# Row-tiled scatter of two images, a streamed router, and a top-2 mixture shared by VectorE, ScalarE and GpSimd

## The chip, the core and the metric

The kernel runs on one core of one Trainium2 chip as one program. The metric is the device time of the whole execution in microseconds (us). Before the change it is 9376.89 us, the median of three runs (9366.43 to 9382.52). Names of the engines as the profile has them: PE is TensorE's matmul side and PEld its weight loads, DVE is VectorE, ACT is ScalarE, POOL is GpSimd, and SP is the engine that issues most of the DMAs.

## The reference

Four layers of a network run over 4 images of 48 x 48 positions with 128 channels, 9216 tokens in all. Each layer adds a mixer of positions and then a per-token part to the running `x`. The change touches two kinds of per-token part.

Layers 1 and 2 end in an expert-choice layer: 64 experts each take a weighted sum over an image's tokens (`topv` is zero but for 8 tokens of each expert), run it through a small network, and give their outputs back to the tokens with the same weights. This giving back is the scatter:

```python
weighted = jnp.einsum('beo,bke->bkeo', out, topv).reshape(Bn, K * E, O)
outputs = outputs.at[jnp.arange(Bn)[:, None], flat_idx].add(weighted)
```

Layer 3 ends in a mixture of 8 experts, of which every token uses the two with the highest router probability:

```python
router_probs = jax.nn.softmax(x @ router_w + router_b, axis=-1)
top_p, top_i = jax.lax.top_k(router_probs, K)
top_p = top_p / jnp.sum(top_p, axis=-1, keepdims=True)
expert_out = jnp.einsum('bnd,edc->bnec', x, expert_w) + expert_b
gathered = jnp.take_along_axis(expert_out, top_i[..., None], axis=2)
return jnp.einsum('bnk,bnkc->bnc', top_p, gathered)
```

The input of both is the layer-normed `x`, and all arithmetic is float32.

## The kernel before, in words

`metaformer` runs the stages one after another. A stage is one or more blocks; at the end of a block all engines meet and the block's semaphores are cleared, so nothing of one block runs beside the next. `X`, the running `x` of layers 1 to 3, stays on chip as 72 tiles of 128 tokens by 128 channels (36 groups of two tiles).

**The scatter** (`scatter_tokens`, called by `expert_choice` in layers 1 and 2). `weights` holds, for two images at a time, 64 rows (experts) of one image in partitions 0 to 63 and 64 rows of the other in 64 to 127. SP moves the experts' outputs into `rows` in the same layout, 16 DMAs (L2287). DVE adds the second bias to the rows of two images (L2307) and lets PE begin. PE then works image by image, in 5 steps per image: a step fills one PSUM bank with 4 tiles (2 in the last) by matmuls with only 64 rows of contraction (L2299). DVE adds each bank to `X` (L2313), 20 additions. PE may run 8 banks ahead.

**The mixture** (`top2_experts`) has these blocks:

- `load_all` fetches the identity, the router and the expert weights, and `bias_rows` fetches the router's and the experts' biases in a load block of its own, then a second block makes from them a row in high and low parts and a matrix of ones, so that a bias can be added by a matmul.
- `norm_and_turn` norms the tokens and leaves them transposed in `XT` (channels by tokens).
- Router block `mr`, 18 turns with 4 tiles each: ACT copies 512 columns of `XT` to `stage` (L3035), PE makes for each tile a matmul with the 128 x 128 token tile as stationary operand and the router's 8 columns as moving one (L3045), and one for the bias (L3046), and DVE copies 32 columns to `gates` (L3055).
- `route` turns `gates` into the normed probabilities of each token's two best experts; all others become 0.
- Mixture block `me`, 36 turns with 2 tiles each: ACT rounds the tokens to `high` (L3079), POOL makes `low` as the rest (L3071), PE makes for each tile and each half of the 8 experts (4 experts by 128 channels, one bank) three matmuls, high by high, high by low and low by high (L3094), and one for the bias (L3095). DVE then takes 8 times, once for each expert, `x = ps * gate + x` per tile (L3112), 16 instructions a turn. Two sets of 4 banks alternate, and so do two buffers each of `high` and `low`.

The order inside a block is the order of the code on each engine. Loops with `Fori` are loops on the chip and others are written out.

## Time and profile before

| | us |
|---|---|
| median of the runs | 9376.89 |
| profiled execution, its own time | 9381.17 |
| its span, first to last instruction | 9378.6 |
| first scatter, PE's first to DVE's last instruction | 6648.6 to 6678.0 |
| second scatter | 8624.0 to 8653.5 |
| load and making of the bias rows | 9083.0 to 9092.7 |
| norm and transposes for the mixture | 9092.7 to 9126.5 |
| router block | 9128.1 to 9175.0 |
| route | 9175.8 to 9193.6 |
| mixture block, ACT's first to DVE's last instruction | 9194.5 to 9361.4 |
| store of the result | 9362.4 to 9378.6 |

The profile is of one execution. Its times are microseconds from the start of the span. Busy time of an engine doesn't say that the engine bounds a stage; for that one reads who waited for whom there. The mean of an instruction (in ns) holds its own start-up, part of which lies beside the instruction before it, so instructions that follow each other closely start at a smaller distance than their duration.

### The profile page before, as it was taken

Reading aid. Unit: us, or ns where it says so; the run is one execution under the profiler, and the core shown is the slowest. Engines: PE = TensorE matmul, PEld = TensorE weight load, DVE = VectorE, ACT = ScalarE, POOL = GpSimd, SP = SyncE. Lnnn points to the kernel's source line nnn. Section 1 sums busy time; section 2 is a strip of 40 time slices with the busy share of each in tenths; the row PEclk is TensorE's granted clock in tenths of the full one; section 3 lists DMA queues with packets and bytes.
Section 4 is the critical chain, followed back from the end, with each engine's and each line's share of the span. In section 5 each row is a group of like instructions: output and inputs, shape, how many; then the busy total and the mean of one; then the engine's idle time right before and its main releaser. Section 6 shows DMA issues by size and latency. Waiting matters only on the chain. (4 is left out here: it accounts for less than half of the span.)

```text
span 9378.6 us, 167204 instructions
## 1 busy us (share of the span) xinstructions
PE 7377.9 (79%) x63268; PEld 4812.3 (51%) x63268; DVE 6500.1 (69%) x8252; ACT 4637.2 (49%) x8709; POOL 4163.0 (44%) x2920
## 2 busy tenths in 40 slices
PE   5877778777778777875799999388499989995667
PEld 3444444444444344444788888166355555553455
DVE  7999899998999799993166555232376656633447
ACT  4666566665666466652156555124224444452431
POOL 4999599995999499983300000000100000010001
PEclk8999999999999999995699999699679999997778
DMA  4555355553555355544332333621300010003000
GB/s 145 165 165 165 92 177 164 163 151 119 165 165 165 91 175 165 165 128 151 134 74 60 89 86 86 160 71 45 143 21 16 21 36 16 16 1 148 21 23 20
DMA packets 470862, 976.30 MB, mean 104 GB/s; under 512 B 127918, under 2 KB 226549, under 8 KB 452983
## 3 DMA queue, kind: packets, MB, share of 16 engines
q1 hardware_dynamic: 469098, 938.10, 33.6%
q10 hardware_dynamic: 960, 27.53, 1.1%
q8 instruction: 501, 8.21, 0.4%
q14 instruction: 303, 2.47, 0.1%
HBM read 822.05 MB, written 114.81 MB: 100 GB/s over the span
## 5 line engine op out<-in xcount | busy, mean ns | idle before, releaser
L892 POOL TENSOR_TENSOR ss_work<-ss_dtu,ss_ringb 128x768 f32<-128x768 f32 x1536 | 2759.6, 1822 | 260.0 <-POOLq L59 256.6
L754 PE MATMUL ss_ps<-ss_work,ss_ident 128*128 128x512 f32 (+1 forms) x6144 | 2307.9, 521 | 615.5 <-POOL ss_work L902 600.0
L754 PEld LDWEIGHTS ss_ps<-ss_work,ss_ident 128*128 128x128 f32 x6144 | 1201.0, 203 | 1503.5 <-issue 1319.0
L876 DVE TENSOR_TENSOR_SCAN ss_work<-ss_ps,ss_last,ss_work 128x768 f32<-128x768 f32 x1024 | 1808.6, 1800 | 64.2 <-ACT ss_ps L807 53.2
L807 ACT ACTIVATE ss_ps<-ss_dt,ss_a_neg 128x768 f32<-128x768 f32 x1536 | 1374.6, 895 | 288.1 <-DVE ss_work L876 270.9
L861 DVE TENSOR_TENSOR ss_work<-ss_work,ss_ps 128x1152 f32<-128x1152 f32 x768 | 1019.0, 1327 | 1.2 <-ACT ss_ps L815 1.2
L2655 DVE TENSOR_REDUCE at_top<-at_ps 128x1 f32<-128x384 f32 x1512 | 728.1, 546 | 402.5 <-PE at_ps L2573 402.3
L2636 ACT ACTIVATE at_probs<-at_ps 128x768 f32<-128x768 f32 x864 | 653.6, 808 | 660.4 <-PE at_ps L2592 659.4
L876 DVE TENSOR_TENSOR_SCAN ss_work<-ss_ps,ss_work 128x768 f32<-128x768 f32 x512 | 878.1, 1742 | 51.4 <-issue 18.0
L1409 DVE COPY mb_mix<-mb_ps 128x432 f32<-128x432 f32 x1088 | 634.4, 632 | 400.5 <-PE mb_ps L1432 400.4
L1499 ACT ACTIVATE mb_mix<-mb_ps 128x432 f32<-128x432 f32 x1088 | 612.6, 619 | 435.0 <-PE mb_ps L1432 429.0
L902 POOL TENSOR_TENSOR ss_work<-ss_work,ss_ringc 128x384 f32<-128x384 f32 x768 | 772.4, 1006 | 22.1 <-DVE ss_work L876 22.1
L1432 PE MATMUL mb_ps<-mb_taps,mb_mats 105*128 105x216 f32 x4352 | 668.1, 298 | 28.8 <-DMA mb_mats<-fq_mats 24.8
L2602 PE MATMUL at_ps<-at_probs,at_v 128*64 128x384 f32 x3456 | 663.5, 506 | 0.0
L1432 PEld LDWEIGHTS mb_ps<-mb_taps,mb_mats 105*128 105x128 f32 x4352 | 549.0, 196 | 128.3 <-issue 78.1
L2558 POOL COPY at_inv<-at_kept 32x384 f32<-32x384 f32 x80 | 39.9, 499 | 1224.3 <-ACT at_kept L2641 1222.7
L1449 PE MATMUL mb_ps<-mb_mix,mb_bins 128*8 128x64 f32 x29376 | 522.3, 221 | 30.7 <-issue 30.5
L1492 POOL COPY mb_bins<-mb_bins_by 128x432 f32<-128x432 f32 x34 | 20.3, 596 | 1182.6 <-PE mb_ps L1449 1049.6
L2573 PE MATMUL at_ps<-at_packs 96*128 96x384 f32 x1512 | 496.9, 379 | 19.6 <-DMA at_packs<-at_high 19.1
L813 ACT ACTIVATE ss_ps<-ss_ringc 128x512 f32<-128x512 f32 x768 | 462.7, 603 | 83.3 <-DVE ss_work L861 80.1
L2592 PE MATMUL at_ps<-at_packs 128*128 128x384 f32 x1728 | 453.0, 355 | 53.2 <-PEq L59 40.2
L1449 PEld LDWEIGHTS mb_ps<-mb_mix,mb_bins 128*8 128x8 f32 x29376 | 420.2, 90 | 94.8 <-issue 36.1
(554 smaller groups left out, 9917.5 us busy)
## 6 DMA issues: line engine op xcount, KB each, us to landing
ss_ringb<-scan_rows SPq DMA_DIRECT2D x768, 384.0 KB, 3.6
ss_ringc<-scan_rows SPq DMA_DIRECT2D x768, 384.0 KB, 3.9
c_w<-in_l_ffn_w SPq DMA_DIRECT2D x52, 1024.0 KB, 12.3
mb_mats<-fq_mats ACTq DMA_DIRECT2D x8, 3360.0 KB, 17.3
at_packs<-at_high SPq DMA_DIRECT2D x64, 288.0 KB, 5.5
fq_mats<-fq_mats_high SPq DMA_DIRECT2D x8, 2048.0 KB, 9.8
fq_bins<-tb_out SPq DMA_DIRECT2D x68, 216.0 KB, 1.9
mb_bins_by<-fq_bins SPq DMA_DIRECT2D x34, 432.0 KB, 3.9
```

What stands on the lines that cost most here:

```text
L754: return pe.matmul(acc[:, d * WIN + a:d * WIN + e], ident[:, :], weighed[:, t % DEEP, d, a:e], start=n == 0 and e - a == 512, stop=n == NS ...
L807: act.activation(decay[d], dt[:, i % 2, d, :], ACT.Exp, scale=a_neg[:, SECTIONS[i][0], d, n:n + 1]).then_inc(s["decayed"], 1)
L861: dve.tensor_tensor(weighed[:, t % DEEP, :, 0:SPLIT], hid[:, t % DEEP, :, 0:SPLIT], bc(spread_c[:, None, :], [P, D2, SPLIT]), ALU.mult).th ...
L876: dve.tensor_tensor_scan(hid[:, t % DEEP, d, ::step], decay[d][:, ::step], drive[:, t % DEEP, d, ::step], start, ALU.mult, ALU.add).then_i ...
L892: pool.tensor_tensor(drive[:, t % DEEP, d, :], dtu[:, t // NST % 2, d, :], ringb[:, t % RING, :], ALU.mult).then_inc(s["driven"], 1)
L902: pool.tensor_tensor(weighed[:, t % DEEP, :, SPLIT:WIN], hid[:, t % DEEP, :, SPLIT:WIN], bc(ringc[:, t % RING, None, SPLIT:WIN], [P, D2, W ...
L1409: copy(*fill_part(h, n)).then_inc(sem, 1)
L1432: ins = pe.matmul(ps[:, n % 4, e * COLS:(e + 1) * COLS], mats[:, first:first + P], taps[:, c % 2, :], start=True, stop=True, skip_group_ch ...
L1449: ins = pe.matmul(ps[32 * g:32 * g + 8, 4 + y % 2, at:at + HALF_E], bins[:, c % 2, n, 1 - m:3 - m, :].rearrange("p m b -> p (m b)"), mix[: ...
L2602: ins = pe.matmul(acc[64 * h:64 * h + 64, 0:R], v[:, j, 2 * pair + h, :, :].rearrange("p a d -> p (a d)"), probs[:, n % 4, h, :], start=j ...
L2636: act.activation(probs[:, n % 4, :, :], ps[:, 2 * (n % 2):2 * (n % 2) + 2, 0:R], ACT.Exp).then_inc(s["weighed"], 1)
L2655: dve.tensor_reduce(top[:, bass.ds(tile + h * NT_, 1), u], ps_bank(ps, 5 + g % 3)[:, 0:R], AX.X, ALU.max).then_inc(s["reduced"], 1)
```

## The change

**Scatter.** The loop goes over pairs of images. In each step one matmul for the lower image (partitions 0 to 63) and one for the upper (64 to 127) alternate, and they fill two different banks. DVE's additions come in the same order. Their number and sizes stay.

**Bias rows.** `bias_rows` is not called for the mixture. The router's bias is fetched to all partitions by one DMA in the first load, and DVE adds it to the logits. The experts' biases come through the gates: 16 small DMAs put them on the diagonal blocks of `blocks` (16 tiles by 8 experts in the partitions), the gates of 16 tiles are transposed by PE, and one matmul then makes gate times bias for 4 tiles.

**Router.** `logits_of_tokens` turns the operands round: the router's 8 columns are stationary and 512 tokens stream past them. Four such matmuls go to four column positions (PSUM partitions 0, 32, 64, 96) of one bank. ACT copies the bank, PE transposes it in 4 pieces, and DVE picks the 8 useful columns out of each 32 and adds the bias. Before it starts, DVE clears 5 banks and `blocks`. SP sends the 16 DMAs in this block.

**Mixture.** `mix_experts` first transposes the gates, then runs 18 bias matmuls, which DVE adds to `X`. Then come 36 pairs of tiles. The bias matmuls are gone from the loop. DVE takes 4 of the 8 experts as before. ACT multiplies the other 4 with their gates into `scaled`, POOL adds these up in two steps to `sums`, and DVE adds `sums` to `X` one pair later. All is written out, no loop on the chip is left.

The diff, cut to its core; the lines it removes from `top2_experts` stand in the listing above (`spread` gives an access pattern that reads the same row into all 128 partitions; `layout` gives the experts' biases as 8 rows of 128 and no longer as one row):

```diff
-                for j in range(B * 5):
-                    b, n = j // 5, j % 5
-                    half = slice(b % 2 * NE, b % 2 * NE + NE)
+                for i in range(NPAIR * 5):
+                    pair, n = i // 5, i % 5
                     if n == 0:
-                        pe.wait_ge(s["rows_ready"], b // 2 + 1)
-                    if j >= 8:
-                        pe.wait_ge(s["added"], j - 7)
+                        pe.wait_ge(s["rows_ready"], pair + 1)
+                    if i >= 4:
+                        pe.wait_ge(s["added"], 2 * (i - 3))
                     for m in range(4 if n < 4 else 2):
-                        ins = pe.matmul(ps[:, j % 8, m * C:(m + 1) * C], tile_of(weights[half, b // 2, :], 4 * n + m), rows[half, b // 2, :], start=True, stop=True)
+                        for h in range(2):
+                            half = slice(h * NE, h * NE + NE)
+                            ins = pe.matmul(ps[:, (2 * i + h) % 8, m * C:(m + 1) * C], tile_of(weights[half, pair, :], 4 * n + m), rows[half, pair, :], start=True, stop=True)
...
+        router_b, blocks = sb("router_b", [P, NX]), sb("blocks", [P, P // NX, C])
         XT = sb("xt", [P, T])
-        stage = sb("stage", [P, 2, 4, P])
-        load_all(nc, "moe_load", [(ident[:, :], w["ident"]), (router[:, :], w["router"]), (ew[:, :], w["ew"])])
-        ones, (router_b, eb) = bias_rows(nc, ctx, "moe_b", [w["router_b"], w["eb"]])
+        load_all(nc, "moe_load", [(ident[:, :], w["ident"]), (router[:, :], w["router"]), (ew[:, :], w["ew"]), (router_b[:, :], spread(w["router_b"], NX))])
...
+        logits_of_tokens(nc, ps, XT, router, router_b, ident, gates, blocks, w["eb"])
+        route(nc, gates)
+        mix_experts(nc, ctx, ps, X, XT, ident, gates, blocks, ew, ew_high, ew_low)
...
+def logits_of_tokens(nc, ps, XT, router, router_b, ident, gates, blocks, eb):
...
+    with nc.sbuf_tensor("lg_kept", [P, GROUPS_T, CHUNK], F32) as kept:
...
+            @block.tensor
+            def _(pe):
+                pe.wait_ge(s["blank"], 2)
+                for n in range(GROUPS_T):
+                    for c in chunks_in(n):
+                        at = 32 * (c % GROUP)
+                        ins = pe.matmul(ps[at:at + NX, n, :], router[:, :], XT[:, CHUNK * c:CHUNK * (c + 1)], start=True, stop=True, skip_group_check=True)
+                    ins.then_inc(s["made"], 1)
+                for n in range(GROUPS_T):
+                    pe.wait_ge(s["kept"], n + 1)
+                    if n >= 3:
+                        pe.wait_ge(s["gated"], n - 2)
+                    for t in range(GROUP):
+                        ins = pe.transpose(ps[:, GROUPS_T + n % 3, t * P:(t + 1) * P], kept[:, n, t * P:(t + 1) * P], ident[:, :])
+                    ins.then_inc(s["turned"], 1)
             @block.scalar
             def _(act):
+                for n in range(GROUPS_T):
+                    act.wait_ge(s["made"], n + 1)
+                    act.activation(kept[:, n, :], ps[:, n, :], ACT.Copy).then_inc(s["kept"], 1)
             @block.vector
             def _(dve):
+                dve.memset(ps[:, 0:GROUPS_T, :], 0.0).then_inc(s["blank"], 1)
+                dve.memset(blocks[:, :, :], 0.0).then_inc(s["blank"], 1)
+                for n in range(GROUPS_T):
+                    g = len(chunks_in(n))
+                    dve.wait_ge(s["turned"], n + 1)
+                    out = gates[:, 16 * n:16 * n + GROUP * g, :].rearrange("p (g t) e -> p t g e", t=GROUP)
+                    source = ps[:, GROUPS_T + n % 3, :].rearrange("p (t g e) -> p t g e", t=GROUP, g=GROUP)[:, :, 0:g, 0:NX]
+                    dve.tensor_tensor(out, source, bc(router_b[:, None, None, :], [P, GROUP, g, NX]), ALU.add).then_inc(s["gated"], 1)
+            @block.sync
+            def _(sp):
+                sp.wait_ge(s["blank"], 2)
+                for k in range(P // NX):
+                    sp.dma_start(blocks[NX * k:NX * (k + 1), k, :], eb).then_inc(s["diagonal"], 16)
+                sp.wait_ge(s["diagonal"], 16 * (P // NX))
...
+def mix_experts(nc, ctx, ps, X, XT, ident, gates, blocks, ew, ew_high, ew_low):
+    PAIRS_T, QUADS_T = G, G // 2
...
+    def rows_in(n):
+        return NX * min(16, 2 * G - 16 * n)
+    def quad_bank(i):
+        return ps[:, (GROUPS_T + i) % 8, :]
+    def expert_bank(v, t, n):
+        return ps[:, 4 * (v % 2) + 2 * t + n, :]
...
+        @block.tensor
+        def _(pe):
+            for n in range(GROUPS_T):
...
+                ins = pe.transpose(ps[0:rows, n, 0:P], gates[:, 16 * n:16 * n + rows // NX, :].rearrange("p t e -> p (t e)"), ident[:, :])
+                ins.then_inc(s["turned"], 1)
+            pe.wait_ge(s["kept_t"], GROUPS_T)
+            for i in range(QUADS_T):
+                n, rows = i // 4, rows_in(i // 4)
+                if i >= 8:
+                    pe.wait_ge(s["bias_added"], i - 7)
+                pe.matmul(quad_bank(i), gates_t[0:rows, n, :], blocks[0:rows, 4 * (i % 4):4 * (i % 4) + 4, :].rearrange("p t c -> p (t c)"),
+                          start=True, stop=True, skip_group_check=True).then_inc(s["bias_made"], 1)
+            pe.wait_ge(s["weights_ready"], 1)
+            for v in range(PAIRS_T):
+                pe.wait_ge(s["lowered"], v + 1)
+                for t in range(2):
+                    if v >= 2:
+                        pe.wait_ge(s["freed"], 2 * (v - 2) + t + 1)
+                        pe.wait_ge(s["scaled"], 2 * (v - 2) + t + 1)
+                    elif t == 0:
+                        pe.wait_ge(s["bias_added"], QUADS_T)
+                    for n in range(2):
+                        for turn, (x, m) in enumerate(((high, ew_high), (high, ew_low), (low, ew_high))):
+                            ins = pe.matmul(expert_bank(v, t, n), x[:, v % 2, t, :], m[:, n * 512:(n + 1) * 512], start=turn == 0, stop=turn == 2)
+                        ins.then_inc(s["made"], 1)
+        @block.scalar
+        def _(act):
+            def stage(v):
+                at_least(act, s["made"], 4 * (v - 1))
+                act.activation(high[:, v % 2, :, :].rearrange("c t p -> c (t p)"), XT[:, 256 * v:256 * (v + 1)], ACT.Copy).then_inc(s["staged"], 1)
+            def scale(v, t):
+                act.wait_ge(s["made"], 4 * v + 2 * t + 2)
+                at_least(act, s["halved"], 2 * (v - 2) + t + 1)
+                for e in range(SHARE):
+                    gate = gates[:, 2 * v + t, SHARE + e:SHARE + e + 1]
+                    ins = act.activation(scaled[:, v % 2, t, e, :], expert_bank(v, t, 1)[:, e * C:(e + 1) * C], ACT.Copy, scale=gate)
+                ins.then_inc(s["scaled"], 1)
+            for n in range(GROUPS_T):
...
+                act.wait_ge(s["turned"], n + 1)
+                act.activation(gates_t[0:rows, n, :], ps[0:rows, n, 0:P], ACT.Copy).then_inc(s["kept_t"], 1)
+            act.activation(ew_high[:, :], ew[:, :], ACT.Copy).then_inc(s["cut"], 1)
+            stage(0)
+            stage(1)
+            for v in range(PAIRS_T):
+                scale(v, 0)
+                scale(v, 1)
+                if v + 2 < PAIRS_T:
+                    stage(v + 2)
+        @block.gpsimd
+        def _(pool):
+            def lower(v):
+                pool.wait_ge(s["staged"], v + 1)
+                source = XT[:, 256 * v:256 * (v + 1)].rearrange("c (t p) -> c t p", t=2)
+                pool.tensor_tensor(low[:, v % 2, :, :], source, high[:, v % 2, :, :], ALU.subtract).then_inc(s["lowered"], 1)
+            def add_up(v):
+                for t in range(2):
+                    pool.wait_ge(s["scaled"], 2 * v + t + 1)
+                    pool.tensor_tensor(scaled[:, v % 2, t, 0:2, :], scaled[:, v % 2, t, 0:2, :], scaled[:, v % 2, t, 2:4, :], ALU.add).then_inc(s["own"], 1)
+                for t in range(2):
+                    pool.wait_ge(s["own"], 2 * v + t + 1)
+                    at_least(pool, s["added"], 2 * (v - 2) + t + 1)
+                    pool.tensor_tensor(sums[:, v % 2, t, :], scaled[:, v % 2, t, 0, :], scaled[:, v % 2, t, 1, :], ALU.add).then_inc(s["halved"], 1)
+            pool.wait_ge(s["cut"], 1)
+            pool.tensor_tensor(ew_low[:, :], ew[:, :], ew_high[:, :], ALU.subtract).then_inc(s["weights_ready"], 1)
+            lower(0)
+            for v in range(PAIRS_T):
+                if v + 1 < PAIRS_T:
+                    lower(v + 1)
+                add_up(v)
+        @block.vector
+        def _(dve):
+            def weigh(v):
+                for e in range(SHARE):
+                    for t in range(2):
+                        if e == 0:
+                            dve.wait_ge(s["made"], 4 * v + 2 * t + 1)
+                        else:
+                            dve.wait_ge(s["summed"], 2 * (SHARE - 1) * v + 2 * (e - 1) + t + 1)
+                        out = tiles[:, 2 * v + t, :]
+                        ins = dve.scalar_tensor_tensor(out, expert_bank(v, t, 0)[:, e * C:(e + 1) * C], gates[:, 2 * v + t, e:e + 1], out, ALU.mult, ALU.add)
+                        ins.then_inc(s["summed"] if e < SHARE - 1 else s["freed"], 1)
+            def add_rest(v):
+                for t in range(2):
+                    dve.wait_ge(s["freed"], 2 * v + t + 1)
+                    dve.wait_ge(s["halved"], 2 * v + t + 1)
+                    out = tiles[:, 2 * v + t, :]
+                    dve.tensor_tensor(out, out, sums[:, v % 2, t, :], ALU.add).then_inc(s["added"], 1)
+            for i in range(QUADS_T):
+                dve.wait_ge(s["bias_made"], i + 1)
+                out = tiles[:, 4 * i:4 * i + 4, :].rearrange("p t c -> p (t c)")
+                dve.tensor_tensor(out, out, quad_bank(i), ALU.add).then_inc(s["bias_added"], 1)
+            dve.wait_ge(s["bias_added"], QUADS_T)
+            for v in range(PAIRS_T):
+                weigh(v)
+                if v:
+                    add_rest(v - 1)
```

How this stands in the order of instructions. SP around the mixture's loads; the first column is the line, `moe_` are the mixture's tensors and `in_` those in memory:

```order
 L312 DMA moe_router<-in_l_ffn_router 128x8
 L312 DMA moe_ew<-in_l_ffn_ew 128x1024
-L308 UNCONDITIONAL_BRANCH
-L309 UNCONDITIONAL_BRANCH
-L312 DMA moe_b_raw<-in_l_ffn_router_b 1x8 x2
-L312 DMA moe_b_raw<-in_l_ffn_eb 1x1024 x2
+L312 DMA moe_router_b<-in_l_ffn_router_b 128x8
 L308 UNCONDITIONAL_BRANCH
 L166 UNCONDITIONAL_BRANCH
+L3081 UNCONDITIONAL_BRANCH
+L3085 DMA moe_blocks<-in_l_ffn_eb 8x128 x16
+L3047 UNCONDITIONAL_BRANCH
```

One load block of four DMAs is gone, one DMA joins the first load, and 16 DMAs come into the router's block.

PE from the end of the norm on, in the kernel before (router block, then mixture block, both loops):

```order
L257 MATMUL moe_ln_ps<-moe_ident,moe_xn 128x128 x72
L165 UNCONDITIONAL_BRANCH
L3037 UNCONDITIONAL_BRANCH
L3040 UNCONDITIONAL_BRANCH
L3040 ISA
L3045 MATMUL moe_ps<-moe_router,moe_stage 128x8
L3046 MATMUL moe_ps<-moe_b_bias,moe_b_ones 128x8
...
L3094 MATMUL moe_ps<-moe_ew_high,moe_stage_high 128x512
L3094 MATMUL moe_ps<-moe_ew_low,moe_stage_high 128x512
L3094 MATMUL moe_ps<-moe_ew_high,moe_stage_low 128x512
L3095 MATMUL moe_ps<-moe_b_bias,moe_b_ones 128x512
```

And PE at the same place in the changed kernel:

```order
L257 MATMUL moe_ln_ps<-moe_ident,moe_xn 128x128 x72
L165 UNCONDITIONAL_BRANCH
L3048 UNCONDITIONAL_BRANCH
L3054 MATMUL moe_ps<-moe_xt,moe_router 8x512 x18
L3061 MATMUL moe_ps<-moe_ident,lg_kept 128x128 x20
L3047 UNCONDITIONAL_BRANCH
L3114 UNCONDITIONAL_BRANCH
L3118 MATMUL moe_ps<-moe_ident,moe_gates 128x128 x4
L3118 MATMUL moe_ps<-moe_ident,moe_gates 64x128
L3125 MATMUL moe_ps<-moe_blocks,moe_gates_t 128x512 x18
L3138 MATMUL moe_ps<-moe_ew_high,moe_stage_high 128x512
L3138 MATMUL moe_ps<-moe_ew_low,moe_stage_high 128x512
```

The router's 144 matmuls became 18 with 20 transposes behind them, and the bias matmuls moved out of the mixture's loop to a stretch ahead of it.

POOL in the mixture's loop of the changed kernel, two pairs of tiles (before, its loop holds L3071 alone):

```order
L3173 TENSOR_TENSOR moe_stage_low<-moe_xt,moe_stage_high 128x256
L3178 TENSOR_TENSOR moe_scaled<-moe_scaled 128x256 x2
L3182 TENSOR_TENSOR moe_sums<-moe_scaled 128x128 x2
L3173 TENSOR_TENSOR moe_stage_low<-moe_xt,moe_stage_high 128x256
L3178 TENSOR_TENSOR moe_scaled<-moe_scaled 128x256 x2
```

The `low` part of a later pair now stands behind the sums of an earlier one.

## Rows read from the trace of the kernel before

**Rows 1.** Windows: length, busy (count) of PE, PEld, DVE, ACT, POOL; clock, DMA.

```profile
6648.50:6678.00 29.50, 29.02 (x144) 28.73 (x144) 12.66 (x22) 0.00 (x0) 0.00 (x0) 0.50 0.01 3
...
9128.00:9175.00 47.00, 45.87 (x216) 45.78 (x216) 3.45 (x18) 11.23 (x18) 0.00 (x0) 0.51 0.00 0
...
9198.80:9204.20 5.40, 5.36 (x13) 4.21 (x14) 0.00 (x0) 0.00 (x0) 0.58 (x1) 0.50 0.00 0
9205.50:9361.40 155.90, 139.29 (x560) 101.99 (x558) 151.60 (x576) 14.13 (x34) 25.12 (x34) 1.00 0.00 0
```

**Rows 2.** Chain that ended last, its shares by line, 9205.5 to the end.

```profile
by line: DVE x L3112 47.6%; issue 26.4%; DVEq L3111 11.5%; DVEq L3112 2.9%; DVEq L3102 1.0%; DVEq L3104 0.4%
```

**Rows 3.** Timeline of the first scatter; start, length, engine, line, what, [idle before, releaser].

```profile
6641.86 10.06 SPq L2287 DMA_DIRECT2D c1s_rows<-c_outs  x16
...
6653.19 0.29 DVE L2307 TENSOR_TENSOR c1s_rows<-c1s_rows,c1s_b 128x128 f32<-128x128 f32 x1 [4.69 <-DMA c1s_rows<-c_outs]
6653.40 1.87 DVE L2313 TENSOR_TENSOR x<-x,c1s_ps 128x512 f32<-128x512 f32 x3
...
6670.63 0.42 DVE L2313 TENSOR_TENSOR x<-x,c1s_ps 128x256 f32<-128x256 f32 x1 [0.17 <-PE c1s_ps L2299]
6671.65 0.69 DVE L2313 TENSOR_TENSOR x<-x,c1s_ps 128x512 f32<-128x512 f32 x1 [0.60 <-PE c1s_ps L2299]
6673.35 0.69 DVE L2313 TENSOR_TENSOR x<-x,c1s_ps 128x512 f32<-128x512 f32 x1 [1.02 <-PE c1s_ps L2299]
...
6677.62 0.42 DVE L2313 TENSOR_TENSOR x<-x,c1s_ps 128x256 f32<-128x256 f32 x1 [0.17 <-PE c1s_ps L2299]
```

**Rows 4.** Line 1222, the matmuls in four tiles: its forms, and a window.

```profile
L1222 PE MATMUL tb_ps<-fq_fa,fq_u x4096: 202/283/323, 4346.8 to 4631.0; 64*36 64x51 f32 x196
...
4352.00:4354.00 2.00, 1.66 (x79) 1.53 (x73) 1.00 1.20 500
```

**Rows 5.** Timeline, load of the bias rows and start of the norm.

```profile
9082.98 0.54 SPq L312 DMA_DIRECT2D moe_b_raw<-in_l_ffn_router_b  x2
...
9092.74 0.06 DVE L184 MEMSET moe_ln_eps<- 128x1 f32 x1 [0.79 <-PEq L59]
```

**Rows 6.** Timeline, first and last instruction of the router block.

```profile
9128.07 1.15 ACT L3035 ACTIVATE moe_stage<-moe_xt 128x512 f32 x2 [1.56 <-PEq L3039]
...
9174.80 0.19 DVE L3055 COPY moe_gates<-moe_ps 128x32 f32 x1 [2.38 <-PE moe_ps L3046]
```

**Rows 7.** Prices from other stages: a clear, by line; the others, timeline of PE.

```profile
L2365 DVE MEMSET at_v<- 128x2304 f32 x1 | 2.0, 1978 | 4.6 <-PEq L59 4.6
...
6488.74 1.97 PE L2099 MATMUL c1w_ps<-c1w_xt,c1w_gate 128*64 128x512 f32 x2
...
6491.23 1.07 PE L2099 MATMUL c1w_ps<-c1w_xt,c1w_gate 128*64 128x512 f32 x2
6492.23 0.65 PE L2091 MATMUL c1w_ps<-c_ident,c_xn 128*128 128x128 f32 x4
...
6613.54 1.07 PE L2193 MATMUL c1e_ps<-c_w,c_pooled 128*32 128x512 f32 x8 [0.19 <-DMA c_w<-in_l_ffn_w]
```

**Rows 8.** Prices for the mixture's loop: groups by line, then PE's timeline.

```profile
L807 ACT ACTIVATE ss_ps<-ss_dt,ss_a_neg 128x768 f32<-128x768 f32 x1536 | 1374.6, 895 | 288.1 <-DVE ss_work L876 270.9 <-PEq L59 17.2
L2636 ACT ACTIVATE at_probs<-at_ps 128x768 f32<-128x768 f32 x864 | 653.6, 808 | 660.4 <-PE at_ps L2592 659.4
L815 ACT ACTIVATE ss_ps<-ss_ringc 128x64 f32<-128x64 f32 x768 | 173.0, 225 | 264.9 <-DVE ss_work L876 249.5
...
L902 POOL TENSOR_TENSOR ss_work<-ss_work,ss_ringc 128x384 f32<-128x384 f32 x768 | 772.4, 1006 | 22.1 <-DVE ss_work L876 22.1
L3071 POOL TENSOR_TENSOR moe_stage_low<-moe_xt,moe_stage_high 128x256 fp32r<-128x256 f32 x36 | 26.5, 738 | 124.8 <-ACT moe_stage_high L3079 124.8
...
9353.56 0.40 PE L3094 MATMUL moe_ps<-moe_ew_high,moe_stage_high 128*128 128x512 f32 x1
...
9354.49 0.39 PE L3094 MATMUL moe_ps<-moe_ew_high,moe_stage_high 128*128 128x512 f32 x1
```

112 lines of the change are left out of this document (31 added, 81 removed).

## The prediction

> **What bounds the kernel now.** I read the windows by stage first, since the change touches stages that run apart from each other. They show the granted clock beside each engine's busy time. In the first scatter (the second is like it) PE is busy for 29.0 of 29.5 us, at a clock of 0.50, which is the 1.2 GHz level [rows 1]. In the router block PE is busy for 45.9 of 47.0 us, also at that level [rows 1]. In the mixture's loop the clock is 1.00 (2.4 GHz) and DVE is busy for 151.6 of 155.9 us [rows 1]. The chain of waits says the same: from 9205.5 on it holds L3112 and DVE's own sequencer and nothing of PE, ACT or POOL [rows 2]. So PE bounds the scatters and the router, DVE the mixture.
>
> **Scatter.** Before, DVE's first addition to `X` starts at 6653.40, since the second row addition, which waits for the last row DMA, stands ahead of it; the last one ends at 6678.04 [rows 3]. PE has 144 records, two for each float32 matmul. Inside an image a bank of 8 records comes every 1.70 us (6671.65 to 6673.35 [rows 3]), 0.213 us a record, which is 256 cycles of 1.2 GHz. Do two row tiles run side by side? Two rows say so. First, where PE passes from the second image (upper rows) to the third (lower rows), the next full bank comes after 1.02 us instead of 1.70 (6670.63 to 6671.65 [rows 3]): the third image's first matmuls ran beside the second's last. Secondly, the matmuls of line 1222, 64 rows by 36 columns, go to four tiles, two by rows and two by columns. 79 of their records take 1.66 us at full clock, 21 ns each [rows 4]. Streaming 51 columns at two cycles for each takes 42 ns at 2.4 GHz, so at least two run at once. I take two at once for the scatter: 72 x 0.213 = 15.3 us of PE from 6648.5 on, ending at 6663.9. DVE's additions start at distances of 0.59 us (three in 1.87 us, the last one 0.69 long) [rows 3] and end at 6653.4 + 16 x 0.59 + 4 x 0.33 = 6664.2 if PE is never late. The two run nearly level, PE fills the last banks last, and I put the end at 6665.2: 12.8 us saved in each, 25.6 in both. If PE came up to full clock, DVE alone would hold it and 13.8 each is saved, 27.6. If each tile waits for the other, nothing is. The new wait, `added` at twice the steps behind, is met: PE reaches the fifth step at 6655.4, and DVE has added the first two banks by 6654.6.
>
> **Bias rows.** The second load begins at 9082.98 and the norm at 9092.74 [rows 5]. Now the norm's block takes the place of the load's: 9.76 us go. The router's bias joins the first load as a fourth DMA, behind the large one; I take 0.5 us for it (about one issue, 0.27 in the row of two, up to 1.0). 9.2 us saved, 8.8 to 9.7.
>
> **Router.** Before, from the first ACT copy at 9128.07 to the end of the last DVE copy at 9174.99 [rows 6]. Now, in order:
> - DVE clears 2560 columns of PSUM and 2048 of `blocks`. At 1978 ns for 2304 columns [rows 7] that is 2.2 + 1.8 = 4.0 us; PE and SP wait for it. DVE can begin some 0.7 us before ACT did, as it waits for the block's start alone: 9127.4, so 9131.4.
> - PE: 5 groups of four column tiles, each 512 columns in two records. The expert layer's four column tiles take 1.07 us for all 8 records [rows 7], against 1.07 us for two records of one tile at that clock and 1.97 at 1.2 GHz [rows 7]; so the four run side by side, and a group costs about 0.9 us at full clock and 1.8 at half. The mixture's PE came up after 5.4 us of work [rows 1], so I take 3 groups at 1.8 and 2 at 0.9: 7.2 us, to 9138.6. All at half clock it is 9.0.
> - The last ACT copy is ready 0.8 us behind (about 600 ns for 512 columns, from 225 for 64 and 808 for 768 [rows 8]). The 20 transposes, 0.6 us for four [rows 7], run partly before it. With DVE's last pick-up I put the end at 9141.5.
> - SP sends 16 DMAs from 9131.4. The scatter's 16 take 10.06 us to issue, and DVE goes on 1.3 us after the last [rows 3]. This gives 9142.8; the bias loads' two in 0.54 us [rows 5] would give 9137.
>
> The block ends at about 9143, against 9175.0: 32 us saved, 29 to 34. `route` is the same.
>
> **Mixture, ahead of the loop.** Before, ACT begins at 9194.5 and DVE's first product at 9205.6, after PE's first four banks at half clock. Now PE transposes the gates and ACT copies them (5 each, 1.7 us), and then come 18 float32 bias matmuls of 512 columns, two records each: 1.8 us at half clock, 0.9 at full one [rows 7]. Three at half clock (5.4 us) and 15 at full come to 18.9 us, then DVE's last addition 0.7. The rounding and POOL's `ew_low` run beside it. PE starts the loop at 9215.9 and not at 9198.8. This is a loss of 17 us, 15 to 31 by the clock. The same work lay behind DVE before.
>
> **Mixture, the loop.** For a pair of tiles:
> - PE: 12 matmuls at 0.231 us (four start in 0.93 us [rows 8]): 2.77 us. Before 16, 3.70.
> - DVE: 8 products instead of 16, at 155.9 / 576 = 0.27 us [rows 1], and two additions of 128 columns, 0.29 us each alone [rows 3]: 2.7 us at most. Before 4.33.
> - ACT: 8 scaled copies of 128 columns. 768 columns cost 808 ns and 64 cost 225 [rows 8], so 128 cost 0.28. A scale from a tile adds 0.09 (895 against 808 ns for 768 columns [rows 8]). That is 0.37 alone and somewhat less in a row; I take 0.33. With the rounding of the next tiles, 3.0 us.
> - POOL: `low` 0.74, two additions of 256 columns 0.74 each, two of 128 at 0.47, by the slope between 738 and 1006 ns [rows 8]: 3.15 us, 3.04 if they overlap a little.
>
> So no engine alone needs more than 3.2 us, but there is a ring. `low` of pair v + 2 stands in POOL's queue behind the sums of pair v, and these wait for ACT's last four copies, which wait for PE's last bank of pair v. From PE's end with v to its start with v + 2: 4 x 0.33 + (0.72 + 2 x 0.44 + 0.72) + three hand-overs of 0.1 = 3.95 us. With v + 2's own 2.77 that is 6.72 us for two pairs, 3.36 each. 35 x 3.36 = 117.6, and the last pair passes all engines, 7.0: 124.6 us after 9215.9, so the end is at 9340.5 instead of 9361.4. 21 us saved. ACT at 0.41 a copy would make 3.65 a pair and save 11; a period of POOL's 3.04 would save 32. PE is at work for 82% of a period, against 85% before at full clock, so I keep the clock.
>
> **Sum.** 25.6 + 9.2 + 32 + 21 = 87.8 us. From the profiled execution's own 9381.2 that gives 9293.4; it lies 4.3 us above the median of the runs, so from 9376.9 it is 9289.
>
> **A rule that speaks against it.** In the loop before, POOL's subtraction takes 738 ns while DVE's products, which read one operand from PSUM, run without a break, and 190 + 2.1 x 256 from the scan's sizes gives the same [rows 8]: these two don't disturb each other. DVE's new additions of `sums` read both operands from SBUF, and no row here shows that beside a POOL instruction. The Trainium skill (SBUF — State Buffer, Who interferes with whom) says that such a Vector instruction contends with a GpSimd one that reads SBUF, and that the one that started first keeps the shared port to its end. What it would make of the time is the first rival.
>
> **Rivals.**
> 1. DVE's additions and POOL's hold each other up. Each of DVE's two keeps POOL out for 0.29 us [rows 3], so a pair costs POOL 3.04 + 0.58 = 3.6 us, and POOL sets the pace. 36 x 0.26 = 9 us more: 9298. For it: POOL is at work for over 90% of the time, so nearly each addition meets it. Against: nothing in the trace. 18%.
> 2. The scatter's row tiles don't overlap, since each has a weight load of 128 columns and those of line 1222 have 36. 25.6 us less saved: 9315. Against: the shorter step between two images. 4%.
> 3. The clock is at the lower level in the loop. 12 x 0.427 = 5.1 us a pair, 36 x 1.76 = 63 us more: 9352. Against: 82% of work against 85% in the row with 1.00, and no gap above 1.2 us. 5%.
> 4. Slower than before: the ring doesn't overlap two pairs at all, each pair passing PE, ACT and POOL in turn. It is 2.77 + 3.95 = 6.7 us a pair, 36 x 3.36 = 121 us more: 9410. It decides from a pair of 3.36 + 88 / 36 = 5.8 us on. For it: two sets of everything, and POOL's fixed order. Against: with the same two sets PE ran a pair ahead of DVE before. 2%.
>
> My forecast has 71%. The chances: a measurement of this kernel tells about 0.2% (19 us) from no change. All cases but the last are faster by more than that, 9352 too; for rest and mistakes in several terms I keep 0.02 for no change: 0.96, 0.02, 0.02.
>
> **The range.** All good ends, 27.6 + 9.7 + 34 + 32 = 103, give 9273; all bad ones, 24 + 8.8 + 29 + 10 = 72, give 9305. A few us for the run and the first two rivals: 9270 to 9309.
>
> **What would show it.** The scatter: PE's 144 records in some 15 us, additions to `X` nearly without waits. Router block: 15 to 16 us, its end with DVE or the 16 DMAs. Bias matmuls: one each 0.9 us after the first few. Loop: DVE's products with waits for PE, POOL with waits for ACT, a pair each 3.3 to 3.4 us. POOL's 128-column additions above 0.6 us, or DVE's above 0.4, would speak for rival 1. I am wrong if PE's records in the scatter keep 0.2 us, or if a pair takes under 3.0 or over 3.7 us.

## The result, and the profile after

| | before | after |
|---|---|---|
| median of four runs, us | 9371.66 (9345.20 to 9382.52) | 9273.26 (9263.69 to 9285.30) |
| profiled execution, its own time | 9381.17 | 9263.69 |
| its span | 9378.6 | 9261.9 |

The ratio is 0.989, with a 95% interval of 0.9871 to 0.9909: the change makes the kernel faster, by 85 to 121 us. The forecast was 88 us. The sign came out, and in the main the mechanism. The median lies 16 us under the predicted 9289.

The windows by stage of the kernel after, in the columns of [rows 1]: the first scatter from its first row DMA, its additions to `X` alone, the second scatter, the router block, PE in it, the bias matmuls (two rows) and the mixture's loop.

```profile
6616.00:6639.90 23.90, 11.09 (x144) 10.29 (x144) 11.47 (x22) 0.00 (x0) 0.00 (x0) 0.79 0.04 9
6628.86:6639.80 10.94, 5.67 (x80) 5.06 (x80) 10.94 (x21) 0.00 (x0) 0.00 (x0) 0.98 0.00 0
8575.30:8598.40 23.10, 11.05 (x144) 10.25 (x144) 11.48 (x22) 0.00 (x0) 0.00 (x0) 0.79 0.04 9
9063.00:9077.40 14.40, 9.60 (x56) 3.41 (x56) 5.35 (x7) 2.98 (x5) 0.00 (x0) 0.65 0.02 5
9067.50:9074.80 7.30, 7.30 (x37) 1.35 (x38) 0.00 (x0) 2.39 (x4) 0.00 (x0) 0.61 0.04 9
9099.10:9103.40 4.30, 4.28 (x5) 1.85 (x6) 1.15 (x2) 1.53 (x3) 3.30 (x3) 0.50 0.00 0
9103.40:9117.40 14.00, 13.98 (x32) 5.76 (x30) 10.57 (x16) 0.00 (x0) 0.42 (x1) 0.98 0.00 0
9118.30:9244.40 126.10, 109.36 (x432) 78.37 (x432) 104.30 (x360) 92.73 (x322) 110.63 (x178) 1.00 0.00 1
```

The reader is to see three things against [rows 1]. PE's 144 records of a scatter take 11.1 us and not 29.0, and DVE, at work for all of 10.94 us, sets the end. In the router block PE needs 7.3 us and not 45.9. In the loop DVE is no longer the full engine, yet none has taken its place: of 126 us POOL is busy for 111, PE for 109, DVE for 104, ACT for 93. With no engine full, waits must hold the pace; the forecast's ring is one candidate, and the runs below test it. The chain of waits over it (its shares by line) runs through POOL, where before it held DVE alone [rows 2]:

```profile
by line: issue 27.8%; POOL moe_sums L3182 22.1%; POOL moe_scaled L3178 17.9%; POOL moe_stage_low L3173 16.3%; PE moe_ps L3138 2.1%; ACT moe_scaled L3152 0.8%; DVE x L3215 0.5%; DVE x L3210 0.5%; POOLq L3111 0.2%; DVEq L3208 0.0%
```

I then laid the timelines of both kernels side by side and measured each stage between the same two instructions. Stages are bounded by starts: "first scatter" from the first row DMA to the next norm, "second" from there to DVE's last addition, "load" from the identity's DMA to the norm, "norm, router" on to `route`, "head" on to PE's first expert matmul, "loop" on to DVE's last addition.

| stage, us | before | after | saved | forecast |
|---|---|---|---|---|
| first scatter | 39.7 | 27.3 | 12.4 | 12.8 |
| second scatter | 35.8 | 22.6 | 13.2 | 12.8 |
| load, bias rows | 14.9 | 5.3 | 9.6 | 9.2 |
| norm, router | 83.0 | 50.9 | 32.1 | 32 |
| route, head of the mixture | 23.1 | 40.0 | -16.9 | -17 |
| loop | 162.2 | 125.9 | 36.3 | 38 |
| sum | 358.7 | 272.0 | 86.7 | 87.8 |
| the stage of line 1302 | 278.0 | 246.4 | 31.6 | 0 |
| all else | 8741.9 | 8743.5 | -1.6 | 0 |

So the terms sum as forecast, and the profiles differ by 30 us more, in a stage that no edit touches: from DVE's first to its last copy of line 1302, ahead of both scatters. Here is a stretch of it in windows, first before, then after (the stage begins at 4393.5 and at 4396.4):

```profile
4400.00:4430.00 30.00, 30.00 (x143) 30.00 (x142) 3.65 (x6) 3.18 (x6) 12.86 (x4) 0.50 0.24 89
```

```profile
4400.00:4430.00 30.00, 25.88 (x577) 25.56 (x579) 7.15 (x12) 6.82 (x13) 18.37 (x6) 0.96 0.65 249
```

The granted clock was 0.50, the 1.2 GHz level, in the one and 0.96 in the other. (The counts differ by more than the clock does, because the slower execution is still in the matmuls of line 1234 for all of this window, 0.21 us each, while the faster one has gone on to the short ones of line 1222.) Is that the change's doing? Repeats answer it.

### The profile page after: what moved, and what is told of

It is laid out like the page before. It is cut to its first block and busy times, and to the rows that moved or that the text cites. A ratio compares the mean times of both kernels' runs of the same rounds, so it can differ in the third digit from the quotient of the medians.

```text
span 9261.9 us, 165385 instructions
## 1 busy us (share of the span) xinstructions
PE 7254.6 (78%) x63005; PEld 4679.2 (51%) x63005; DVE 6461.8 (70%) x8039; ACT 4717.5 (51%) x8987; POOL 4250.9 (46%) x3064
## 5 line engine op out<-in xcount | busy, mean ns | idle before, releaser
L807 ACT ACTIVATE ss_ps<-ss_dt,ss_a_neg 128x768 f32<-128x768 f32 x1536 | 1374.6, 895 | 289.0 <-DVE ss_work L876 272.0
L1432 PE MATMUL mb_ps<-mb_taps,mb_mats 105*128 105x216 f32 x4352 | 669.2, 298 | 29.7 <-DMA mb_mats<-fq_mats 23.3
L2595 PE MATMUL at_ps<-at_packs 128*128 128x384 f32 x1728 | 452.2, 354 | 53.4 <-PEq L59 39.7
```

The source lines that it names most:

```text
L807: act.activation(decay[d], dt[:, i % 2, d, :], ACT.Exp, scale=a_neg[:, SECTIONS[i][0], d, n:n + 1]).then_inc(s["decayed"], 1)
L1432: ins = pe.matmul(ps[:, n % 4, e * COLS:(e + 1) * COLS], mats[:, first:first + P], taps[:, c % 2, :], start=True, stop=True, skip_group_ch ...
```

## Experiments

All ratios are to the kernel before on the same chip. Since whole times of one kernel spread by 20 to 75 us from its lowest to its highest run, most verdicts rest on a stage's length in the profile; each changed stage repeats within 1 us in all profiles of a kernel.

### The same kernels again

The kernel before three times and the changed one twice, with no edit.

> The kernel before, unchanged. The profiles of before and after differ by 116.7 us, of which about 29 us lie ahead of every changed line: in the stage of line 1302 PE is granted 0.50 where the other profile has 0.96. Theory A (that stage's clock comes out differently from execution to execution, whatever the kernel): this kernel's repeats spread over 20 us or more, the ratio is 1.000 within 0.001, and in its profile the stage of line 1302 (DVE's first to last copy, 4398.6 to 4671.5 before, 4399.0 to 4642.8 after) may be of another length than the 273 us of the first profile. Theory B (the changed kernel makes this stage faster, by where its code or its data lie): this profile shows 273 us again, and all profiles of the changed kernel and its parts 244 us.

> The changed kernel, unchanged. Its changed stages save 12.3 + 13.2 (scatters) + 10 (bias rows) + 32 (router block) + 22 (mixture) = 89 us by the two profiles. Theory A (the other 28 us are the clock of an unchanged stage in that one execution): over five rounds the ratio is 1 - 89 / 9370 = 0.9905, within 0.001. Theory B (they belong to the change): 1 - 117 / 9370 = 0.9875.

> The kernel before, unchanged, for another profile of the stage of line 1302. Theory A (its length varies for itself): anywhere in 246 to 282 us, and with the other two repeats the means of both kernels come closer. Theory B (shorter with the change): 270 us or more.

> The same once more. Theory A: one of the two under 270 us. Theory B: both 270 us or more. The changed stages (scatters 39.7 and 35.8, load 15, norm and router 83, loop 162) repeat within 0.5 us in either theory.

> The changed kernel, unchanged, once more. Theory A: the stage of line 1302 anywhere in 246 to 282 us. Theory B: 246 to 265. The changed stages (scatters 27 and 22.6, load 5.4, norm and router 50.6, loop 125.9) repeat within 0.5 us.

| profile | line 1302's stage | changed stages | last addition at |
|---|---|---|---|
| before | 278.0 | 358.7 | 9361.1 |
| before_again | 263.4 | 358.9 | 9340.2 |
| before_c | 248.5 | 358.6 | 9322.5 |
| before_d | 258.2 | 358.4 | 9346.4 |
| after | 246.4 | 272.0 | 9244.1 |
| after_again | 258.8 | 271.1 | 9253.5 |
| after_c | 258.8 | 272.4 | 9246.3 |

Theory A holds. The unedited kernel before has stages of 278 and of 248 us, and the window of the short one (before_c) shows the clock at 0.86, where the first profile of the same code had 0.50:

```profile
4400.00:4430.00 30.00, 22.57 (x571) 22.18 (x570) 7.12 (x12) 6.26 (x12) 14.88 (x5) 0.86 0.71 275
```

One window doesn't tell the stage's length: before_d has 0.50 there too, and 258 us. PE's matmuls in this part of the program do, here in before and then in before_c:

```profile
L1234 PE MATMUL tb_ps<-fq_fe,fq_ax 100*128 100x72 f32 x816 | 168.9, 410 | 3.0 <-ACT fq_ax L1276 3.0
L1222 PE MATMUL tb_ps<-fq_fa,fq_u 64*36 64x51 f32 x4096 | 94.6, 270 | 61.0 <-issue 60.9
```

```profile
L1234 PE MATMUL tb_ps<-fq_fe,fq_ax 100*128 100x72 f32 x816 | 133.5, 348 | 3.0 <-ACT fq_ax L1276 3.0
L1222 PE MATMUL tb_ps<-fq_fa,fq_u 64*36 64x51 f32 x4096 | 94.7, 272 | 62.5 <-issue 62.4
```

So the time that varies is that of line 1234's matmuls alone; the kernel after has the same 133.5 us as before_c. Over all 18 profiles on record the stage's length falls in three heaps (246 to 249, 258 to 263, 276 to 282 us), and both kernels appear in more than one of them: the mean is 262 us in the four profiles of the kernel before and 266 in the twelve of the changed kernel and its variants. This rules out theory B.

Less that stage, the last addition stands at 9083, 9077, 9074 and 9088 before and at 8998, 8995 and 8988 after. The means, 9080.5 and 8993.3, are 87 us apart. The repeats' times: before_again 9367.87 (ratio 0.999, 0.998 to 1.0001), after_again 9278.00 (0.9899, 0.9884 to 0.9914). Over all runs of the two unedited kernels, 64 and 10, the means are 9370.1 and 9278.3 us, with standard deviations of 13 each: 92 us, plus or minus 9 (the sets were run on several chips, and the kernel before has a mean from 9366 to 9376 us on four of them).

### The scatter alone

The diff's part in `scatter_tokens`, on the kernel before.

> The kernel before with the new order of the scatter's matmuls and additions alone. Row tiles side by side: 72 pairs of records in place of 144 in a row, each scatter 12.4 to 13.8 us shorter by the row DMAs' landing, 26 us in both: 9345, ratio 0.9972. From PE's rows: PE 11 us busy instead of 29. Rival (the gain comes from the granted clock, 0.98 in place of 0.50, and not from the tiles): the same length, but a bank's 16 records at 0.213 / 2 = 0.107 us each, 1.7 us for 16, with two tiles side by side at the lower clock, so PE and not DVE sets the pace there; a scatter that still shows 0.085 us a record in the first 64 tells both apart.

Measured: 9350.28 us, ratio 0.9961 (0.9946 to 0.9977); the scatters 27.0 and 23.4 us, 25.1 saved in both. The windows over the first half of the matmuls and the rest tell how much is the tiles' and how much the clock's:

```profile
6653.80:6659.10 5.30, 5.28 (x48) 5.29 (x50) 0.00 (x0) 0.00 (x0) 0.00 (x0) 0.50 0.07 14
6659.10:6672.00 12.90, 6.97 (x98) 6.17 (x96) 11.18 (x21) 0.00 (x0) 0.00 (x0) 0.90 0.00 0
```

At the 1.2 GHz level 48 records took 5.3 us, 0.11 each: half of the 0.213 of before, so two tiles run at once, as forecast. Then the clock rose, which the forecast did not have, and PE was out of the way: the gain is the tiles' and the clock's together.

### Two images alternating, or in groups

```diff
-                    for m in range(4 if n < 4 else 2):
-                        for h in range(2):
-                            half = slice(h * NE, h * NE + NE)
+                    for h in range(2):
+                        half = slice(h * NE, h * NE + NE)
+                        for m in range(4 if n < 4 else 2):
```

> The changed kernel's scatter with the two images' matmuls of a step one image after the other (4 and 4), in place of alternating. Banks, waits and DVE's work are as in the changed kernel, whose scatter takes 23.8 and 23.0 us from the first row DMA to DVE's last addition, with PE 11.1 us busy. Theory T (row tiles run side by side only where neighbouring matmuls are for different ones): PE needs nearly the sum, 144 x 0.107 = 15 us at full clock to 29 us at the lower, from 6.7 us after the first DMA on: the scatter ends 1 to 12 us later, 25 to 35 us each. Rival (the gain is the clock and the banks, not the alternation): the scatter's length stays within 0.5 us.

Measured: 9277.91, ratio 0.9899 (0.9879 to 0.9918); the scatters 28.1 and 22.8 us. Theory T fell. PE is slower in groups (eight records in 1.02 us at the lower level and 0.58 at the upper, against 0.85 and 0.47 alternating), but far from 1.70, and DVE's additions hide the rest (the first scatter is 0.8 us longer than in the changed kernel, 0.7 of it because its rows landed later):

```profile
6635.27 8.95 PE L2300 MATMUL c1s_ps<-c1s_rows,c_weights 64*128 64x128 f32 x72 [9.82 <-DVE c1s_rows L2308]
6641.93 0.29 DVE L2308 TENSOR_TENSOR c1s_rows<-c1s_rows,c1s_b 128x128 f32<-128x128 f32 x1 [6.72 <-DMA c1s_rows<-c_outs]
6642.14 10.97 DVE L2316 TENSOR_TENSOR x<-x,c1s_ps 128x512 f32<-128x512 f32 x20
```

So what counts is that both images' steps stand near each other in the queue; the matmuls need not alternate one by one. The 1.02 us are the same as the step that [rows 3] showed at the passage between two images, on which the forecast was built.

### The router alone

The streamed router on the kernel before, without `blocks`, its clear and its 16 DMAs:

```diff
-        stage = sb("stage", [P, 2, 4, P])
+        rb = sb("router_b", [P, NX])
...
+        logits_of_tokens(nc, ps, XT, router, rb, ident, gates)
         route(nc, gates)
```

> The kernel before with the streamed router and its bias from the load, and nothing else: the bias rows' block stays (the mixture needs it), and the blocks of the expert biases with their clear and their 16 DMAs are not there. Theory (PE's 36 records and the clear of PSUM bound the block): 2.2 us clear, 7.3 us PE, 2.6 us transposes and last addition: 12.3 us from the block's start in place of 47 + 0.7, 35 us less than before: ratio 0.9963. Rival (the 16 DMAs or the second clear bound the changed block): they are gone here, so the block would be shorter than in the changed kernel by more than the 1.8 us of the clear.

Measured: 9344.95 us, ratio 0.9955 (0.9942 to 0.9968); norm and router 48.4 us, 34.6 less than before. It is 2.3 us shorter than in the changed kernel (50.7 in the mean of three), which is the second clear with the gap ahead of it, 9065.24 to 9067.42 in these rows of the changed kernel:

```profile
9063.05 2.19 DVE L3072 MEMSET moe_ps<- 128x2560 f32 x1 [7.20 <-PEq L59]
9065.66 1.76 DVE L3073 MEMSET moe_blocks<- 128x2048 f32 x1 [0.42 <-issue]
9067.45 5.38 SPq L3085 DMA_DIRECT2D moe_blocks<-in_l_ffn_eb  x16
9067.48 7.27 PE L3054 MATMUL moe_ps<-moe_xt,moe_router 128*8 128x512 f32 x36 [7.82 <-DVE moe_blocks L3073]
...
9075.37 1.97 DVE L3079 TENSOR_TENSOR moe_gates<-moe_ps,moe_router_b 128x128 f32<-128x128 f32 x5 [7.95 <-PE moe_ps L3061]
```

The 16 DMAs take 5.38 us to issue, not the 10.06 of the scatter's that I had reckoned with, and the last is issued at 9072.83, before PE's last matmul ends at 9074.75. They bound nothing.

### The mixture: is it the ring or the shared port?

In the loop of the changed kernel: groups by line, with columns as in [rows 8], then the wait of PE's weight loads (us in total, times, longest):

```profile
L3178 POOL TENSOR_TENSOR moe_scaled<-moe_scaled 128x256 f32<-128x256 f32 x72 | 57.5, 807 | 29.6 <-ACT moe_scaled L3152 29.6
L3182 POOL TENSOR_TENSOR moe_sums<-moe_scaled 128x128 f32<-128x128 f32 x72 | 32.4, 469 | 0.0
...
L3210 DVE TENSOR_TENSOR x<-x,moe_sums 128x128 f32<-128x128 f32 x72 | 29.2, 446 | 1.1 <-POOL moe_sums L3182 1.1
```

```profile
PEld moe_ps L3138 <- POOL moe_stage_low L3173: 27.6, 34, 1.2
```

Both are there. PE waits for POOL's `low` 34 times in 36 pairs: the ring. And DVE's additions take 446 ns in the mean, not 292, and POOL's 807, not 738. Their durations fall in three heaps: DVE's near 285, 420 and 824 ns (37, 18 and 17 of 72), POOL's near 735, 785 and 980 (37, 17 and 18). Side by side in the timeline of one pair:

```profile
9184.09 0.49 DVE L3210 TENSOR_TENSOR x<-x,moe_sums 128x128 f32<-128x128 f32 x2
9184.20 0.98 POOL L3178 TENSOR_TENSOR moe_scaled<-moe_scaled 128x256 f32<-128x256 f32 x1 [0.66 <-ACT moe_scaled L3152]
```

POOL's addition, begun while DVE's two run, takes 0.98 us and not 0.74. The other way round, an addition of DVE's that begins 0.11 us behind one of POOL's takes 0.82 us and not 0.29. Here the trace agrees with the Trainium skill (SBUF — State Buffer, Who interferes with whom), whose rule was the first rival's ground: who starts first keeps the shared port.

> The changed kernel with DVE's two additions of sums cut from 128 columns to one (this leaves the upper four experts' share out of 127 of 128 columns; every wait stays). In the changed kernel's loop (125.9 us from PE's first to DVE's last instruction, 3.50 a pair) DVE's additions take 446 ns, against 292 alone, and POOL's additions of 256 columns 807 ns, against 738. Theory P (the two hold each other up, and POOL's lost time sets the pace, through the ring or directly): POOL's 256 columns fall to 740 ns, 2 x 0.07 = 0.14 us a pair, the loop to 120.5. Rival in its full price (0.29 us for each of DVE's two): 3.50 - 0.58 = 2.9 a pair, 105. Theory R (the ring alone, DVE's additions don't matter): 125.9 within 1 us, with POOL's additions as long as before.

```diff
-                    dve.tensor_tensor(out, out, sums[:, v % 2, t, :], ALU.add).then_inc(s["added"], 1)
+                    dve.tensor_tensor(out[:, 0:1], out[:, 0:1], sums[:, v % 2, t, 0:1], ALU.add).then_inc(s["added"], 1)
```

Measured: the loop 121.8 us (9279.73 in all, ratio 0.9905, 0.9885 to 0.9924), POOL's additions at 736 ns:

```profile
L3178 POOL TENSOR_TENSOR moe_scaled<-moe_scaled 128x256 f32<-128x256 f32 x72 | 52.8, 736 | 30.8 <-ACT moe_scaled L3152 29.8
```

Theory P holds at its small price: 4.1 us for the whole loop. Divided by 36 pairs, the loop makes 3.38 us a pair without the hold-up and 3.50 with it, but this holds the ends of the loop too. The forecast's 3.36 is the distance from pair to pair; PE's starts in the middle of the loop (twenty pairs) are 3.32 us apart without the hold-up and 3.44 with it. Now the ring:

> The changed kernel with three buffers for the rounded tiles and the rests instead of two, staged and lowered a pair earlier, so that POOL's low of pair v + 2 stands ahead of the sums of pair v. No engine has less work. Theory R (the ring PE, ACT, POOL, PE over two pairs sets 3.5 us): the ring is cut and POOL runs at its own work, 0.73 + 2 x 0.81 + 2 x 0.47 = 3.28 us a pair: 36 x 3.28 = 118 and 2 to 3 us of the ends, 120 to 121. Rival (POOL's own work sets the pace already, 91% busy, and its waits only move): 125 to 126.

```diff
-            for v in range(PAIRS_T):
-                if v + 1 < PAIRS_T:
-                    lower(v + 1)
+            lower(1)
+            for v in range(PAIRS_T):
+                if v + 2 < PAIRS_T:
+                    lower(v + 2)
                 add_up(v)
```

(with `high` and `low` in three buffers, `v % 3`, and ACT's `stage(v + 3)` in place of `stage(v + 2)`.)

> The changed kernel with POOL's four additions of a pair joined into two (512 and 256 columns) and DVE's two into one of 256. POOL's work falls from 3.28 to 0.73 + 1.27 + 0.74 = 2.74 us a pair, but from ACT's last copy to the next low it is 1.27 + 0.74 + 0.73 = 2.74, in place of 0.74 + 0.9 + 0.73 = 2.4. Theory R (ring): 4 x 0.29 + 2.74 + 0.3 + 2.77 = 6.97 us for two pairs, 3.5 each: 125 us, no gain. Rival (POOL's own work sets the pace): 2.8 to 2.9 a pair, 103 to 107.

```diff
-                for t in range(2):
-                    pool.wait_ge(s["scaled"], 2 * v + t + 1)
-                    pool.tensor_tensor(scaled[:, v % 2, t, 0:2, :], scaled[:, v % 2, t, 0:2, :], scaled[:, v % 2, t, 2:4, :], ALU.add).then_inc(s["own"], 1)
+                pool.wait_ge(s["scaled"], 2 * v + 2)
+                part = scaled[:, v % 2, :, :, :]
+                pool.tensor_tensor(part[:, :, 0:2, :], part[:, :, 0:2, :], part[:, :, 2:4, :], ALU.add).then_inc(s["own"], 1)
```

(and so for the narrow additions, and DVE's.)

> Three buffers and the joined additions together. With the ring cut every engine goes by its own work: PE 2.77, POOL 2.74, ACT 8 x 0.288 + 0.43 = 2.73, DVE 8 x 0.27 + 0.45 = 2.6. Theory R: a pair in 2.8 to 3.0 us, the loop 103 to 110, the kernel 16 to 23 us below the changed one. Rival (the engines hold each other up on their memory): every instruction of POOL's and DVE's gets longer, and a pair stays above 3.2, 117 us or more.

> Three buffers, and DVE's additions of sums cut to one column (the upper experts' share is left out of the rest, as in the run with two buffers). With two buffers the cut took 4.1 us off the loop (125.9 to 121.8); with three buffers the loop takes 110.8, DVE waits for PE 2.8 us in all, and its additions of sums take 543 ns. Theory P (with the ring cut, DVE and the hold-up by POOL set the pace): DVE loses 2 x 0.5 us of work a pair, and the next bound is PE's 2.77 or POOL's 0.73 + 2 x 0.74 + 2 x 0.46 = 3.1 less overlap of 0.07 a record: 2.85 to 2.95 a pair, 103 to 107. Rival (POOL's own work sets 3.08 already): 109 to 111.

| kernel | loop, us | loop / 36, us | whole, us | ratio to before |
|---|---|---|---|---|
| after | 125.9 | 3.50 | 9273.26 | 0.989 (0.9871 to 0.9909) |
| no_rest | 121.8 | 3.38 | 9279.73 | 0.9905 (0.9885 to 0.9924) |
| three_stages | 110.8 | 3.08 | 9278.56 | 0.9914 (0.9889 to 0.9939) |
| wide_sums | 134.4 | 3.73 | 9294.39 | 0.9914 (0.9888 to 0.9940) |
| three_wide | 108.4 | 3.01 | 9281.99 | 0.9893 (0.9859 to 0.9927) |
| three_norest | 115.6 | 3.21 | 9269.90 | 0.9897 (0.9879 to 0.9915) |

The whole times can't rank these: 15 us in the loop are less than what line 1302's stage varies by (247.5 in the profile of three_stages, 280.8 in that of wide_sums). The loops can. Two results decide for the ring. With no engine's work changed, three buffers take 15 us off. And with POOL's work cut by half a microsecond a pair, wide_sums is 8.5 us slower, since its one wide addition starts only after ACT's last copy and so lengthens the way round:

```profile
L3178 POOL TENSOR_TENSOR moe_scaled<-moe_scaled 128x512 f32<-128x512 f32 x36 | 52.6, 1462 | 43.5 <-ACT moe_scaled L3152 43.1
```

A smaller busy time made the loop slower. I had expected no gain there, but not a loss: the addition takes 1.46 us and not the 1.27 worked out, as DVE's additions meet 35 of the 36 (the one that none meets takes 1.29).

In three_wide, with the ring cut and the additions joined, the theory holds at its slow end: 108.4 us, where it had 103 to 110. Its rival, that the engines hold each other up, is there in part: DVE's joined addition takes 0.85 us in the mean where 0.45 was expected, but a pair stays below the rival's 3.2 us.

Once the ring is cut, DVE and POOL both run without a pause, and the port is part of their pace. In three_stages a pair takes 3.03 us there (from 9145 to 9225 neither engine has a gap): DVE's eight products and its two additions, which take 1.03 us for the two and not 0.58, while POOL's instructions follow each other without a gap:

```profile
9179.80 1.03 DVE L3212 TENSOR_TENSOR x<-x,moe_sums 128x128 f32<-128x128 f32 x2
9179.86 0.82 POOL L3179 TENSOR_TENSOR moe_scaled<-moe_scaled 128x256 f32<-128x256 f32 x1
9180.64 0.93 POOL L3183 TENSOR_TENSOR moe_sums<-moe_scaled 128x128 f32<-128x128 f32 x2
...
9180.75 2.15 DVE L3204 SCALAR_TENSOR_TENSOR x<-moe_ps,moe_gates,x 128x128 f32<-128x128 f32 x8
9181.54 0.73 POOL L3174 TENSOR_TENSOR moe_stage_low<-moe_xt,moe_stage_high 128x256 fp32r<-128x256 f32 x1
9182.24 1.47 POOL L3179 TENSOR_TENSOR moe_scaled<-moe_scaled 128x256 f32<-128x256 f32 x2
9182.82 1.04 DVE L3212 TENSOR_TENSOR x<-x,moe_sums 128x128 f32<-128x128 f32 x2
```

My expectation of 120 for it was too high: it gave POOL 3.28 us of work a pair, but its records overlap a little, and it did a pair in 3.03 to 3.08.

three_norest missed both theories, which had at most 111 us. Most of its pairs take 2.80 us, PE's own pace, but four times PE stands still for 1.7 to 2.3 us. The cause is in this timeline of DVE and POOL:

```profile
9145.58 1.42 POOL L3179 TENSOR_TENSOR moe_scaled<-moe_scaled 128x256 f32<-128x256 f32 x2
9146.08 3.93 DVE L3212 TENSOR_TENSOR x<-x,moe_sums 128x1 f32<-128x1 f32 x2
...
9146.97 0.87 POOL L3183 TENSOR_TENSOR moe_sums<-moe_scaled 128x128 f32<-128x128 f32 x2
...
9147.80 0.73 POOL L3174 TENSOR_TENSOR moe_stage_low<-moe_xt,moe_stage_high 128x256 fp32r<-128x256 f32 x1
...
9148.50 1.42 POOL L3179 TENSOR_TENSOR moe_scaled<-moe_scaled 128x256 f32<-128x256 f32 x2
...
9150.09 0.87 POOL L3183 TENSOR_TENSOR moe_sums<-moe_scaled 128x128 f32<-128x128 f32 x2 [0.16 <-DVE x L3212]
```

An addition of one column, 0.15 us alone, took 3.86 us (its row above joins it with the next one). Seven instructions of POOL's ran meanwhile, one under way and six behind it, without a gap, and the addition ended when POOL stopped to wait for it (0.16 us idle before 9150.09). DVE's products behind it came late, and so PE had no free bank: each of the four times its next matmul starts 0.10 us after the product that frees the bank. After two of the four pauses seven of PE's matmuls took 0.63 us each in place of 0.40, as at the lower clock (0.64 and 0.63 in these stretches). So the hold-up can last for several instructions of the other engine. It is not the rule: thirteen other additions of this run that were held up took 0.77 us, and those of 0.82 us in three_stages ended after one instruction of POOL's, although POOL ran on without a gap. What makes the difference stays open.

### Without the bias matmuls

The changed kernel with 1 of 18 bias matmuls and additions ahead of the loop, which leaves out the biases of all tiles but four. DVE's additions and the waits for them are cut like the matmuls in the edit shown.

> The changed kernel with one of the 18 bias matmuls and of DVE's 18 additions ahead of the loop (the experts' biases are left out for all tiles but four). In the changed kernel they run from 9099.1 to 9118.1 and PE starts the loop at 9118.3, at full clock. Theory W (the prologue also warms PE up): the loop starts 17 us earlier, by POOL's ew_low, at 2.6 + 1.4 us after the transposes, but its first 4 to 6 us of PE work pass at the lower clock, some 2 to 3 us longer: 14 us saved in all. Rival (the loop is bound by the ring and doesn't feel the clock of its first pairs): 16 to 17 us saved.

```diff
-                if i >= 8:
-                    pe.wait_ge(s["bias_added"], i - 7)
+                if i:
+                    continue
```

Measured: route and head 24.9 us in place of 40.0, the loop 127.8 in place of 125.9: 13.1 us saved by stages (9274.25 in all, ratio 0.9891, 0.9875 to 0.9907; a difference of 13 us doesn't show in the whole times). Theory W holds. The loop's first matmuls pass at a mean clock of 0.75, where the changed kernel's start at 1.00 (9118.3 to 9121.3):

```profile
9136.00:9144.50 8.50, 7.71 (x24) 5.86 (x24) 3.93 (x15) 4.40 (x16) 3.65 (x7) 0.75 0.01 2
```

### What the runs point to, together

Three buffers in the mixture; in the scatters the 16 row DMAs issued half by SP and half by ACT, and the additions to `X` for the first two images ahead of the second row addition; in the router block PE waits for the first clear alone.

> All that the runs point to: three buffers in the mixture (loop 110.8 in place of 125.9); in the scatters the additions of the first two images ahead of the second row addition, and the 16 row DMAs issued half by SP and half by ACT; in the router block PE waits for the first clear alone. Scatter: DVE starts at 6.7 / 2 + 1 = 4 to 5 us after the first DMA, in place of 12.9, and needs 20 x 0.55 = 11 us: 16 us each in place of 23.4, 14 to 15 in both. Router: 2.2 us less. Sum 15 + 14.5 + 2.2 = 32 us below the changed kernel, 0.9865 of the kernel before. Rival for the scatters (DMAs issued by two queues land no sooner): DVE starts at 6.7, 18 us each, 11 in both.

```diff
-                for q in range(NPAIR):
-                    dve.wait_ge(s[f"moved{q}"], 16 * GE * 2)
-                    dve.tensor_tensor(rows[:, q, :], rows[:, q, :], b2[:, :], ALU.add).then_inc(s["rows_ready"], 1)
                 for i in range(NPAIR * 5):
                     pair, n = i // 5, i % 5
+                    if n == 0:
+                        dve.wait_ge(s[f"moved{pair}"], 16 * GE * 2)
+                        dve.tensor_tensor(rows[:, pair, :], rows[:, pair, :], b2[:, :], ALU.add).then_inc(s["rows_ready"], 1)
```

Measured: 9253.97 us (9234.22 to 9271.50), ratio 0.9874 (0.9856 to 0.9892). The loop and the router gave what was expected (110.8; 48.1 for norm and router), the scatters little, 5.9 us where 11 to 15 were expected: 23.3 and 20.7 us from the place where SP's first row DMA stands (ACT's first is issued 1.16 us ahead of it). The two queues did land the rows sooner: the first row addition comes 4.98 us after the first row DMA, and 6.35 in the changed kernel. But DVE's additions to `X` begin after 7.45 us and not after 4 to 5. Two things were missed. With DVE at hand early, PE at the lower clock sets the pace of the first ten additions. And PE then waited for the second row addition:

```profile
6644.49 0.29 DVE L2317 TENSOR_TENSOR c1s_rows<-c1s_rows,c1s_b 128x128 f32<-128x128 f32 x1
6644.83 4.51 PE L2307 MATMUL c1s_ps<-c1s_rows,c_weights 64*128 64x128 f32 x72 [2.04 <-DVE c1s_rows L2317]
```

> The combined version with DVE's second row addition ahead of the fourth step instead of the sixth. In the combined version PE waits 2.0 us for it, behind DVE's ten additions for the first two images, though the rows landed before. Theory: PE goes on without that wait, each scatter 1.5 to 2 us shorter, 3 to 4 us in all: 9250. Rival (DVE's 20 additions and PE's lower clock in the first 5 us set the end): no more than 0.5 us each.

```diff
-                    if n == 0:
-                        dve.wait_ge(s[f"moved{pair}"], 16 * GE * 2)
-                        dve.tensor_tensor(rows[:, pair, :], rows[:, pair, :], b2[:, :], ALU.add).then_inc(s["rows_ready"], 1)
+                    if i in (0, 3):
+                        q = min(i, 1)
+                        dve.wait_ge(s[f"moved{q}"], 16 * GE * 2)
+                        dve.tensor_tensor(rows[:, q, :], rows[:, q, :], b2[:, :], ALU.add).then_inc(s["rows_ready"], 1)
```

Measured: 9250.33 us (9200.13 to 9275.30), ratio 0.9863 (0.9835 to 0.9891); the scatters 22.0 and 18.1, 3.9 us less in the two together, as the theory had it. PE's wait is 0.18 us now:

```profile
6662.89 4.51 PE L2307 MATMUL c1s_ps<-c1s_rows,c_weights 64*128 64x128 f32 x72 [0.18 <-DVE c1s_rows L2318]
```

Its changed stages add up to 244.1 us, against 272.0 after and 358.7 before. It is the fastest version by its median and by its stages. By whole times alone it is not set apart: its interval overlaps that of the changed kernel's repeat (0.9884 to 0.9914) in 0.0007 and nearly covers that of best.

## Why the forecast came out as it did

**The scatter.** Right in what it is worth (25.6 us forecast, 25.6 measured), but by two errors that cancel, and wrong in what ends last. I put PE at half clock through to the end, level with DVE. The rows show 26 records in 2.90 us at 0.50 and then 0.96 (scatter_only came up only after 5.3 us):

```profile
6622.70:6625.60 2.90, 2.90 (x26) 2.90 (x28) 0.00 (x0) 0.00 (x0) 0.00 (x0) 0.50 0.07 13
6625.60:6628.10 2.50, 2.50 (x42) 2.31 (x38) 0.00 (x0) 0.00 (x0) 0.00 (x0) 0.96 0.08 15
```

So the case "DVE alone holds it" came, worth 27.6 by the forecast. The missing 2 us: I took the landing of the rows from the first scatter of [rows 3], where DVE's additions begin 11.54 us after the first row DMA. After the change they begin after 12.87 and 12.00 us; the second scatter of the kernel before has 12.2 to 12.7 itself.

**Bias rows.** 9.6 against 9.2 us. The fourth DMA cost some 0.2 us, and not 0.5.

**Router.** 32.1 against 32. The parts came out near too: clears 4.0 us forecast and 4.4 with the gap between them, PE 7.2 and 7.3. The end was misjudged: I gave it to the 16 DMAs, 15.6 us after the start of DVE's clear, and it came with DVE's last pick-up after 14.3. The saving still fits by luck, for the clear starts 1.0 us later than I had assumed: 35.6 us after the norm's first instruction, 0.3 behind where ACT's first copy stood before and not 0.7 ahead.

**Head of the mixture.** 16.9 against 17 us lost. The bias matmuls came to full clock after five records; six were assumed. no_bias shows that only 13 us of it can be had back, since this work also brings the clock up for the loop.

**The loop.** From PE's first to DVE's last instruction's end it takes 126.2 us against 124.6, and from pair to pair 3.44 us against 3.36. The ring that the forecast named is the mechanism: no_rest has 3.32 without the hold-up at the port, and cutting the ring frees 15 us. The first rival's mechanism is there too, so the two were not alternatives as I had set them. Its size was wrong: I charged it 0.58 us a pair, 9 us in all; it costs 0.11 to 0.12 a pair, 4 us. Only half of DVE's additions meet one of POOL's (35 of 72), and most of the lost time falls on DVE, which had 0.6 us a pair to spare (104 us of 126).

**The sum.** Forecast 87.8, measured stage by stage 86.7, by profiles less the varying stage 87, by the means of all runs 92 plus or minus 9. The step of the prediction that failed is the last one, from the sum to the time: the starting value, and the term "a few us for the run" in the range. I took the profile's own time and the median of three runs, 9376.9, as fixed. The kernel's own spread is larger: its 64 runs range from 9341 to 9396 us with a standard deviation of 13, their mean is 9370.1, and one unedited stage alone, that of line 1302, took 248 to 278 us in four profiles of this kernel, by the clock that was granted to the matmuls of line 1234. Of the 16 us between 9289 and 9273.26, 7 lie in the starting value (from 9370.1 the same sum gives 9282.3) and 5 in the four runs of the changed kernel, whose ten runs have a mean of 9278.3. The last 4 are inside the plus or minus 9. The first comparison taken by itself says 103 us, 85 to 121, an interval nearly as wide as my whole range of 39 us. A measurement that wide can fall at the edge of the range or past it with every term of the sum right; the range should have carried the spread of the runs on top of that of the terms. Whether a few microseconds are a true gain outside the changed stages stays open: 92 plus or minus 9 doesn't tell 87 from 98.

## What to carry to other kernels

In a loop that several engines share, work out the way round (who waits for the last piece of whom, through each queue's order) before the busy times: here one buffer more, with no work saved, was worth 15 us of 126, and fewer instructions on the busiest engine made it slower.

Before a difference between two profiles is explained, line them up stage by stage and run the old kernel again: a quarter of this difference lay where nothing was changed.

## What the runs showed of the hardware that I had not expected

- With one 64-row tile at work at a time, PE was busy for 29.0 of 29.5 us and stayed at 0.50 [rows 1]; with two side by side the same matmuls came up to 0.96 after 2.9 us (5.3 us before the rise in scatter_only, whose only edit this is). It was so each time: in all ten scatters with the old order (five profiles) the clock is 0.50 from PE's first to its last record, in all 26 with the new order (thirteen profiles, grouped among them) its mean is 0.68 to 0.89. Packing the array gave the clock as well as the overlap.
- The matmuls of line 1234 (100 rows by 128 columns, 72 streamed) took 168.9 us in one execution and 133.5 in another of the same code, as they were granted 0.50 for a longer or a shorter part; those of line 1222 beside them took 94.6 and 94.7. The stage's length was 246 to 282 us over 18 profiles.
- DVE's addition of one column waited for 3.86 us while seven POOL instructions ran without a gap, four times in one run. Most hold-ups at the port lasted for one instruction.
